# Splitting attention weights into narrow parts: two steps on GpSimd instead of VectorE, and their stores in SyncE's queue

## The reference

```python
xq = _div_clamp_fp8(x, in_scale)                              # x rounded to fp8
return jnp.einsum('bsi,oi->bso', xq * in_scale, wq) * w_scale
```

## Time and profile before

| | |
|---|---|
| median of 3 runs | 709.66 us (709.24 to 710.46) |
| profiled execution | 709.97 us, its span 707.9 us |
| TensorE busy | 619.0 us (87%), 4521 instructions |
| VectorE busy | 556.7 us (79%), 1354 |
| ScalarE busy | 421.7 us (60%), 1370 |
| GpSimd busy | 262.3 us (37%), 355 |
| TensorE's granted clock, mean | 0.959 |

### The profile page before, as it was taken

One profiled execution on the slowest core, in us unless ns is written; L12 is line 12 of the kernel. 1 busy time (PEld: TensorE's weight loads), 2 busy tenths in 40 slices (PEclk: granted clock), 3 DMA queues, 4 the chain that ended last, 5 costly groups with the idle time before them and its releaser, 6 DMA issues.

```text
span 707.9 us, 13476 instructions
## 1 busy us (share of the span) xinstructions
PE 619.0 (87%) x4521; PEld 490.5 (69%) x4567; DVE 556.7 (79%) x1354; ACT 421.7 (60%) x1370; POOL 262.3 (37%) x355
## 2 busy tenths in 40 slices
PE   4347989989889999999999999999999999989936
PEld 3236766766767877777687777777787788776724
DVE  7998688979676857979788578797874777877697
ACT  4246757656777736666767365668563667663531
POOL 3203553433224553334335634333332455440231
PEclk9557999999999999999999999999999999999978
DMA  8245843673463222222232232232243243220001
GB/s 268 68 172 180 305 156 111 225 194 133 129 182 106 87 90 97 97 98 97 98 112 97 98 98 98 98 98 97 98 157 97 98 98 98 98 31 1 1 0 59
DMA packets 38398, 80.09 MB, mean 113 GB/s; under 512 B 3486, under 2 KB 28730, under 8 KB 33594
## 3 DMA queue, kind: packets, MB, share of 16 engines
q1 hardware_dynamic: 38144, 79.21, 34.6%
q10 hardware_dynamic: 186, 0.02, 0.0%
HBM read 66.62 MB, written 12.60 MB: 112 GB/s over the span
## 4 chain that ended last, share of the span: by engine, by line
PE 55%; DVE 32%; issue 6%; ACT 5%; POOL 2%; DMA 0%; DVEq 0%; ACTq 0%
PE bank L695 13%; PE bank L571 11%; PE bank L675 9%; PE bank L578 6%; PE bank L644 4%; PE bank L719 3%; DVE Cb L1702 3%; PE bank L661 2%; DVE nm L1687 2%; PE bank L676 2%; PE bank L709 1%; POOL rs L1276 1%; DVE Cb L1717 1%; DVE Cb L1718 1%; DVE rest L1644 1%
## 5 line engine op out<-in xcount | busy, mean ns | idle before, releaser
L695 PEld LDWEIGHTS bank<-V,Pt 128*128 128x128 f32 x1024 | 126.4, 191 | 38.3 <-DVE Cb L1702 25.8
L695 PE MATMUL bank<-V,Pt 128*128 128x129 f32 x1024 | 137.9, 278 | 9.3 <-DVE Cb L1702 7.6
L1027 ACT ACTIVATE square<-bank 128x128 bf16<-128x128 f32 x372 | 98.5, 277 | 71.2 <-PE bank L571 43.6
L675 PE MATMUL bank<-QT,KTt 128*128 128x512 f32 x256 | 133.9, 605 | 2.0 <-POOL diag L1290 1.6
L1010 ACT ACTIVATE Pt<-bank 128x512 f32<-128x512 f32 x128 | 76.8, 600 | 73.3 <-remote 48.0
L1687 DVE TENSOR_REDUCE nm<-bank 128x2 f32<-128x512 f32 x128 | 82.0, 682 | 31.1 <-PE bank L661 31.0
L1276 POOL TENSOR_TENSOR rs<-ve,mhalf 128x6 f32<-128x6 f32 x64 | 94.5, 1476 | 5.3
L1290 POOL TENSOR_TENSOR diag<-identb,nm 128x512 bf16<-128x512 bf16 x64 | 67.1, 1049 | 74.1 <-DVE nm L1687 74.1
L571 PE MATMUL bank<-WQ,xq 128*128 128x256 f32 x496 | 77.5, 300 | 6.7 <-DVE nm L1687 4.5
L1702 DVE SCALAR_TENSOR_TENSOR Cb<-bank,ro,ism 128x128 bf16<-128x128 f32 x256 | 78.1, 347 | 4.5
L571 PEld LDWEIGHTS bank<-WQ,xq 128*128 128x128 f32 x496 | 65.6, 192 | 19.1 <-DVE nm L1687 13.9
(11 more groups left out here) (235 smaller groups left out, 1100.7 us busy)
## 6 DMA issues: line engine op xcount, KB each, us to landing
WQ<-wq_split SPq DMA_DIRECT2D x29, 1024.0 KB, 7.7
WH<-wh_split SPq DMA_DIRECT2D x29, 384.0 KB, 9.0
ism<-smooth_inverse SPq DMA_DIRECT2D x32, 256.0 KB, 6.5
wq_split<-stage SPq DMA_DIRECT2D x6, 1024.0 KB, 3.9
wst<-in_L_xattn_wproj SPq DMA_DIRECT2D x16, 256.0 KB, 3.8
wh_split<-stageh SPq DMA_DIRECT2D x6, 384.0 KB, 5.5
wst<-in_L_xattn_wq SPq DMA_DIRECT2D x8, 256.0 KB, 4.4
wst<-in_L_xattn_wqx SPq DMA_DIRECT2D x8, 256.0 KB, 4.6
```

The lines of the kernel that those rows point to most:

```text
L675: nc.tensor.matmul(o[:], KTt[u % 2][:, x, t * P:(t + 1) * P], QT[u % 2][:, x, :], start=True, stop=False)
L695: last = nc.tensor.matmul(o[:, h * (P + 2):h * (P + 2) + P + 1], Pt[:, x, k, h * S + t * P:h * S + (t + 1) * P], V[u % 2][:, x, k, 0:P + 1 ...
L1027: last = A(square[:, t, h], head(t, h), ACT.Square, accum_out=ss[:, t, h:h + 1])
```

## The change

VectorE's cast and subtraction of n = 2 move to a new GpSimd function `narrow_parts(g)`, called at eight places of its program: (0) and (1) after the last layer norm power of the head, (2) after norm(1, 0), (3), (4), (6), (7) behind powers(u + 1, 1) in units 0, 1, 4, 5, and (5) after half(3) in unit 2. `store_weights(g)` is split into `store_wide(g)`, which waits for the high and low parts, and `store_thin(g)`, which waits for `wr_ready`; each has its own semaphore (`wq_stored`, `wh_stored`) and its own place in SyncE's list. Loads wait for both.

```diff
-            def store_weights(g):
+            def store_wide(g):
 
                 sp.wait_ge(s["w_evac"], 8 * (g + 1))
                 sp.wait_ge(s["wl_ready"], 3 * (g + 1))
+                sp.dma_start(wq_dram[g], halves_of(g)[0][:].bitcast(F32).rearrange("p a k c -> p (a k c)")
+                             ).then_inc(s["wq_stored" if g >= 2 else "wq01_stored"], 16)
+
+            def store_thin(g):
+
                 sp.wait_ge(s["wr_ready"], g + 1)
...
+                sp.dma_start(wh_dram[g], halves_of(g)[1][:].rearrange("p a k c -> p (a k c)")
+                             ).then_inc(s["wh_stored" if g >= 2 else "wq01_stored"], 16)
...
                 if u < G:
                     sp.wait_ge(s["wq01_stored"], 64)
-                    sp.wait_ge(s["wq_stored"], 32 * (g - 1))
+                    sp.wait_ge(s["wq_stored"], 16 * (g - 1))
+                    sp.wait_ge(s["wh_stored"], 16 * (g - 1))
...
-            store_weights(2)
+            store_wide(2)
             weights(4)
-            store_weights(3)
+            store_thin(2)
+            store_wide(3)
             weights(5)
             for u in range(UNITS):
                 if u and u + 1 < UNITS:
                     load_smooth(u + 1)
                 if u == 0:
                     load_weights(2)
+                    store_thin(3)
                     load_weights(3)
-                    store_weights(4)
+                    store_wide(4)
                 elif u != 1 and u + 2 != G - 1 and u + 2 < UNITS:
                     load_weights(u + 2)
                 if u == 1:
                     weights(6)
+                    store_thin(4)
                 if u == 2:
-                    store_weights(5)
+                    store_wide(5)
                     weights(7)
+                    store_thin(5)
                 if u == 3:
-                    store_weights(6)
+                    store_wide(6)
                     load_out_weights(0)
+                    store_thin(6)
                 if u == 4:
-                    store_weights(7)
+                    store_wide(7)
                 if u == 5:
                     load_out_weights(2)
                     load_out_weights(4)
+                    store_thin(7)
...
-                    if g >= 3 and n == 0:
-                        act.wait_ge(s["wq_stored"], 32 * (g - 2))
+                    if g >= 3 and n in (0, 2):
+                        act.wait_ge(s["wh_stored" if n else "wq_stored"], 16 * (g - 2))
...
+            def narrow_parts(g):
+
+                pool.wait_ge(s["wl_ready"], 3 * (g + 1))
+                if g >= 3:
+                    pool.wait_ge(s["wh_stored"], 16 * (g - 2))
+                thin = halves_of(g)[1]
+                chain.add(gp.tensor_copy(thin[:, 1], rest[:]))
+                chain.wait()
+                gp.tensor_tensor(thin[:, 2], rest[:], thin[:, 1], ALU.subtract).then_inc(s["wr_ready"], 1)
...
+                if u in NARROW_BEHIND:
+                    narrow_parts(NARROW_BEHIND[u])
...
-                        dve.wait_ge(s["wq_stored"], 32 * (g - 2))
+                        dve.wait_ge(s["wq_stored"], 16 * (g - 2))
...
-                    if n == 2:
-                        ch.wait()
-                        dve.wait_ge(s["wl_ready"], 3 * (g + 1))
-                        link(v.tensor_copy(thin[:, 1], rest[:]))
-                        v.tensor_tensor(thin[:, 2], rest[:], thin[:, 1], ALU.subtract
-                                        ).then_inc(s["wr_ready"], 1)
```

More of the change, by code:

```diff
@@ L235, in build_program @@
             ((5, OUT_W), (6, OUT_W), (7, OUT_W)))
+        NARROW_BEHIND = {0: 3, 1: 4, 4: 6, 5: 7}
         def round_of(u, i):
@@ L278, in build_program @@
             "x_loaded x_rest_loaded ctx_loaded rows_loaded vecs_loaded kern_loaded bias_loaded smooth_loaded wst0_loaded "
-            "wst1_loaded wp0_loaded wp1_loaded ism0_loaded ism1_loaded w3_loaded wo_loaded rw_loaded smooth_stored wq_stored wq01_stored "
+            "wst1_loaded wp0_loaded wp1_loaded ism0_loaded ism1_loaded w3_loaded wo_loaded rw_loaded smooth_stored wq_stored wh_stored wq01_stored "
             "wq0_loaded wq1_loaded out_stored "
@@ L372, in load_weights @@
                     sp.wait_ge(s["wq01_stored"], 64)
-                    sp.wait_ge(s["wq_stored"], 32 * (g - 1))
-                else:
-                    sp.wait_ge(s["wq_stored"], 32 * (G - 2))
+                    sp.wait_ge(s["wq_stored"], 16 * (g - 1))
+                    sp.wait_ge(s["wh_stored"], 16 * (g - 1))
+                else:
+                    sp.wait_ge(s["wq_stored"], 16 * (G - 2))
+                    sp.wait_ge(s["wh_stored"], 16 * (G - 2))
                 sp.dma_start(WQ[u % 2][:].bitcast(F32).rearrange("p a k c -> p (a k c)"), wq_dram[g]
@@ L396, in _ @@
             weights(3)
-            store_weights(0)
+            store_wide(0)
+            store_thin(0)
             sp.wait_ge(s["smooth_inverted"], 1)
             sp.dma_start(smooth_dram.rearrange("(p c) -> p c", p=P), smooth_inv[:]).then_inc(s["smooth_stored"], 16)
-            store_weights(1)
+            store_wide(1)
+            store_thin(1)
             sp.wait_ge(s["smooth_stored"], 16)
@@ L1302, in _ @@
             norm(0, 2)
+            narrow_parts(0)
+            narrow_parts(1)
             powers(0, 0)
@@ L1305, in _ @@
             norm(1, 0)
+            narrow_parts(2)
             half(0)
@@ L1371, in _ @@
                     half(u + 1)
+                if u == 2:
+                    narrow_parts(5)
                 if u == UNITS - 3:
```

## The result

| | before | after |
|---|---|---|
| median, 20 runs each, side by side | 709.33 us | 711.35 us |
| profiled execution, its span | 709.97, 707.9 us | 712.22, 710.4 us |
| VectorE busy | 556.7 us | 552.3 us |
| GpSimd busy | 262.3 us | 275.9 us |
| TensorE's granted clock, mean | 0.959 | 0.976 |

The account below looks back on a forecast made before the run. VectorE was taken to matter only where the critical chain (TensorE 55%, VectorE 32%) runs through it. Gains -7.35, ports +1.9, late load +2.9 make -2.55 us: 707.4 from 709.97, as median 707.1 us; range 703.9 to 711.5.

Parts of the forecast that it names:

- the second rival: Unit 4: TensorE idles 5.9 us and the clock falls, 2.1 us lost; +1.85 us, 711.5 us; chance 0.15.
- What VectorE is rid of, in the units: Gains without VectorE's cast and subtraction: unit 1 1.95 us, unit 2 1.0, unit 3 1.15, unit 4 to 5 1.15.
- The head: Before unit 0: 2.1 us gained from groups 0 to 2, 1.0 port cost for group 1; unit 0 about 1.1 earlier.
- The collision of group 1: Head: narrow_parts(1) beside VectorE's fp8 steps costs 1.0 us, between 0 and 1.65.
- That of group 0: Head: group 0 meets operations that read PSUM, or a wait, so its port cost is 0.
- GpSimd's durations: On GpSimd, a 128x512 cast takes about 0.61 us and a subtraction 1.04; 1.7 us per group with the wait.
- Ports, group 4: Unit 1: narrow_parts(4) beside VectorE's quantisation and scans costs 0.6 us, between 0 and 1.65.
- group 7 the two terms: Unit 4 to 5: 1.15 us gained on VectorE, 0.3 us port cost.
- The load of unit 6: Ahead of project(6, 0): load behind store_thin(6), TensorE waits 3.6 us (2.0 to 5.9), of which 2.9 us count.
- the first rival: Load no obstacle: wait of 2.0 us, 1.3 counting, port cost 0.5; -5.5 us, 704.1 us; chance 0.18.
- The clock behind it: After the wait for load 6: a low clock costs 2.1 us, from a wait of 3.9 us on.
- Split stores: SyncE's queue: the wide store's earlier release helps nobody; loads wait for earlier thin stores, load 5 at most 1.5 us late.

Follow-up runs that it names:

- e5: Changed kernel with narrow_parts(4) moved behind half(2) in unit 1, clear of the scans; 708.68 us against 709.2, ratio 0.9995.
- e8: Changed kernel with narrow_parts(6) ahead of powers(5, 0), narrow_parts(4) behind half(2), and groups 0, 1 and 2 made by VectorE; 704.67 us against 709.2, ratio 0.9934.
- e9: Changed kernel with narrow_parts(6) ahead of powers(5, 0) and narrow_parts(4) behind half(2), nothing else; 704.48 us against 709.0, ratio 0.9928.
- e11: Changed kernel with narrow_parts(6) ahead of powers(5, 0), narrow_parts(4) behind half(2), and group 1 alone made by VectorE; 704.28 us against 709.0, ratio 0.9931.
- e1: Changed kernel with narrow_parts(6) called ahead of powers(5, 0) in unit 4; 707.14 us against 709.14, ratio 0.9959.
- e6: Changed kernel with 10 scratch matmuls on TensorE filling the wait for load 6; 710.16 us against 709.2, ratio 1.0011.
- e3: Changed kernel with GpSimd's cast and subtraction cut to 4 columns of each 256, waits and stores kept; 705.04 us against 709.14, ratio 0.9939.
- e4: Changed kernel with only the stores split and moved, VectorE making all narrow parts; 708.93 us against 709.14, ratio 0.9995.
- e2: Changed kernel with 18 scratch matmuls on TensorE ahead of the wait for load 6; 714.6 us against 709.14, ratio 1.0063.
- e10: As e7, with store_thin(1) placed behind store_wide(2) in SyncE's list; 703.75 us against 709.0, ratio 0.9915.
- e7: Changed kernel with narrow_parts(6) ahead of powers(5, 0), narrow_parts(4) behind half(2), narrow_parts(1) held until the fp8 steps are done; 708.26 us against 709.2, ratio 0.9982.

## Why the prediction was wrong

The sign was wrong; the time, 711.35, lies at the edge of the range, and that of the second rival, 711.5, but by other terms: a wait of 4.5 us and not of 5.9, and a second low clock in unit 1, which no rival had. That the time came out inside the range is partly luck. Step by step:

- **What VectorE is rid of, in the units.** Right in the main. Turn 3 to 4 gave 1.44 us (1.0 forecast), turn 4 to 5 1.26 (1.15), and e5, where narrow_parts(4) is out of the way, 1.58 in turn 1 to 2 (1.95). There GpSimd's product of unit 1 (L1268), which had stretched the subtraction, now meets VectorE's next step, 0.72 us instead of 0.41: that part of the 0.77 us did not go, it moved.
- **The head.** -1.1 was forecast, -0.28 is what the one profile shows, and by e8, e9 and e11 the trade is worth nothing measurable. The collision of group 1 was sized rightly (1.07 us against 1.0). That of group 0 was put at 0: beside it two VectorE steps took 1.02 and 0.60 us where before has 0.73 and 0.16. And VectorE waited 0.42 and 0.56 us for GpSimd's two powers near the end of the head, where I had counted one such wait. The heads of equal code differ too: turn 0 began at 59.21 in e1 and 60.77 in e9. A profile's head alone can't carry a term of 1 us.
- **GpSimd's durations.** The cast was right (0.61 us). The subtraction takes 1.16 us, not 1.04: I took it from a product of the same shape. For group 6 that is 0.1 us of the thin store's lateness.
- **Ports, group 4.** 0.6 us was taken; the scans alone lost 1.34. This is the first mis-sized term of turn 1 to 2. The value lay inside the bounds of 0 and 1.65, and the row nearest to it, 0.77 us more on a subtraction, spoke for more than 0.6: one instruction stretched by 0.77, while here two GpSimd instructions met VectorE's. For group 7 the two terms together were right: turn 5 to 6 of e9 is 0.85 shorter than before, and 1.15 - 0.3 is that. By the Trainium skill ("SBUF — State Buffer", Who interferes with whom) the port pair goes to one of the two for a whole instruction; this trace agrees roughly: the uint16 step of the head, 0.43 us alone, ended at 48.02, 0.28 behind the end of GpSimd's subtraction. The scans lost less than by that rule: a block by what was left of the cast (94.01 to 94.56) and by a whole subtraction would cost them 0.55 + 1.16 = 1.7 us; they lost 1.34, and GpSimd lost 0.17 + 0.26.
- **What the collision did next.** Not foreseen. The move itself took away the first of TensorE's two waits (1.52 us); the collision lengthened the second, 1.27 us in e5, to 2.60, and the clock fell behind it: 1.2 us more (0.9 + 0.3, by e1). I had priced the port in VectorE's time only.
- **The load of unit 6.** The place, the chain and its times were right: thin store landed 2.5 us after its issue (2.9 forecast), load 6 issued 2.6 us behind store_thin(6) (2.95). The landing of WH was mis-sized, 9.8 us against 8.3, though the median of 9.0 stood in the prediction as the case against the first rival. So the wait was 4.53 us, not 3.6. The share of it that counts was too small as well. Behind turn 5, project(6, 0) started 4.77 us later in after than in e1 (9.00 against 4.23), and turn 5 to 6 is 6.4 us longer, of which 2.0 is the clock: 4.4 us of lateness counted, 0.35 were absorbed, not 0.7. In e5 and e6 it is 0.35 too (4.66 us late cost 4.3, 4.21 cost 3.9); e3, with most of GpSimd's work left out, doesn't fit (2.21 us late cost 1.3). The term of 2.9 us measured 4.4.
- **The clock behind it.** Its price was right, 2.1 forecast, 2.0 measured in after by e6 (1.5 in e3 and e5). Its condition was wrong, and with it the forecast, which had 0 for this term. I let it decide from 3.9 us on, the length of the one gap I had looked at the earlier trace rows. A gap of that length shows that the clock is low behind 3.9 us; it shows nothing of shorter ones. e3 has it behind 1.96 us, and before itself has it behind 1.87 us, at 638 to 640 us, in a part of the trace that I took for alike in both kernels and left aside. So the forecast of 3.6 us, had it come true, would probably have met the low clock as well, and 0.48 for a case without it was too much.
- **The step that failed**, in short: the load of unit 6 was given 2.9 us with the clock at 1.00; it cost 4.4 us and 2.0 more for the clock. The collision of group 4 with the clock behind it came second, 0.6 us forecast, 2.5 measured (1.3 + 1.2).
- **Split stores.** Right: no cost and no gain by themselves (e4).

With sizes as measured the sum stands: against before, head -0.3, turn 1 to 3 +0.9, turn 3 to 5 -2.7, turn 5 to 6 +5.5, in all +3.5 us at the last turn (634.17 against 630.64), of which the last turn's stretch gave back 1.0. That is the clock behind the wait of 1.87 us, low in the one profiled execution and not in the other, and no work of the change. The medians are 2.0 us apart.

## What to carry to other kernels

Before a step moves to another engine, ask what its result releases: here its own duration hardly mattered, but it stood behind an unrelated power, and a store behind it in the DMA queue held back a load that had no room. Two calls moved (narrow_parts(6) forward, narrow_parts(4) away from the scans) turned a loss of 0.2% into a gain of 0.7%. And give a new wait of TensorE a chance of the clock on top of its length: in these profiles, behind the head, none of the waits of 1.5 to 1.7 us was followed by a low clock, 5 of the 13 of 1.87 us were, the one of 1.96, 3 of the 4 of 2.6 and both of 4.4 to 4.5, for 1.1 to 2.0 us each time. A forecast can look for such rows in the whole trace, not only near the change.

## What was not expected of the hardware

- The granted clock can fall after TensorE has resumed: e3, wait of 1.96 us, at 1.00 for the first microsecond of work, then 0.50; before, wait of 1.87 us up to 636.70, at 1.00 in 637 to 638 and 0.50 in 638 to 640. Behind waits of 2.6 us it fell in after, e2 and e6 and held in e1. The Trainium skill ("TensorE: Matmul & The Clock Gate", What's actually happening) has the clock depend on TensorE's activity; these rows agree as far as that, and none says why e1 differs.
- VectorE and GpSimd can slow each other at once: two scans took 2.60 us instead of 1.26 beside a cast and a subtraction, which themselves took 0.78 and 1.42 us instead of 0.61 and 1.16.
- The landing time of a transfer of one size spans a wide range: 384 KB landed 2.5 us after issue with only one load behind it (store_thin(6)), 5.5 and 9.8 behind 1024 KB (load 6 in e1 and in after), and 1024 KB 3.9 to 10.2 us (store_wide(2) in e10 and e7). Why e1's load took 5.5 us and after's 9.8, with the same amount ahead of it, isn't settled. In after the load of load_smooth, issued at 154.14, was still moving (it landed 7.6 us after its issue); in e1 it was issued 5 us ahead of load 6. The other profiles go with that: 8.6 to 9.8 us where it was issued 2.2 us ahead (after, e3, e5, e6), 5.3 to 5.5 where 4.6 us or more (e1, e7 to e11). No run changed it alone.
